# A gated cross-attention layer with routed experts: another start, another order of late loads, and x's normalisation of units 2 to 5 on GpSimd

## What is computed

```python
x = x + tanh(g_xattn) * attention(layernorm(x), ctx)     # 16 heads of 16, 77 context rows, masked
x = x + tanh(g_ffn) * ffn(layernorm(x))
# ffn: softmax(xf @ gate_w.T) -> the best 2 of 4 experts, weights rescaled to sum 1
y = sum over the 2 chosen e of w_e * (silu(xf @ eg[e].T) * (xf @ eu[e].T)) @ ed[e].T
y = y + (silu(xf @ sg.T) * (xf @ su.T)) @ sd.T           # the shared expert
```

## Time and profile before

| | |
|---|---|
| median of 3 runs | 926.68 us (924.75 to 927.69) |
| the profiled execution | 928.73 us, its span 926.8 us |
| busy in the span | TensorE 879.2 us (95%), VectorE 579.7 (63%), ScalarE 478.2 (52%), GpSimd 468.4 (51%) |
| mean granted clock of TensorE | 0.99 of 2.4 GHz |
| chain that ended last, by engine | TensorE 80%, ScalarE 7%, VectorE 6%, issue 3%, DMA 2%, GpSimd 1% |

### The profile page before, as it was taken

One profiled execution on the slowest core, in us unless ns is written; L12 is line 12 of the kernel. 1 busy time (PEld: TensorE's weight loads), 2 busy tenths in 40 slices (PEclk: granted clock), 3 DMA queues, 4 the chain that ended last, 5 costly groups with the idle time before them and its releaser, 6 DMA issues.

```text
span 926.8 us, 22188 instructions
## 1 busy us (share of the span) xinstructions
PE 879.2 (95%) x6635; PEld 786.4 (85%) x6636; DVE 579.7 (63%) x1294; ACT 478.2 (52%) x1804; POOL 468.4 (51%) x644
## 2 busy tenths in 40 slices
PE   6788999999999999799999999999999999999995
PEld 4557788878887899799989999999999999999994
DVE  4788899999988589478654444444444444444442
ACT  2999999999998344366533232323232222222221
POOL 4476667667647334466324444444444444444442
PEclk9899999999999999899999999999999999999998
DMA  7124322223212221333322222222222222222222
GB/s 207 35 78 121 111 87 92 86 63 112 74 59 92 92 76 59 97 99 113 121 58 40 39 41 37 42 37 43 36 44 35 44 35 44 34 45 34 45 34 24
DMA packets 56864, 61.74 MB, mean 67 GB/s; under 512 B 15642, under 2 KB 45183, under 8 KB 56799
## 3 DMA queue, kind: packets, MB, share of 16 engines
q1 hardware_dynamic: 42871, 43.15, 14.8%
q0 software_dynamic: 12864, 17.57, 11.8%
q10 hardware_dynamic: 1064, 0.21, 0.1%
HBM read 34.78 MB, written 25.82 MB: 65 GB/s over the span
## 4 chain that ended last, share of the span: by engine, by line
PE 80%; ACT 7%; DVE 6%; issue 3%; DMA 2%; POOL 1%; SPq 0%; DVEq 0%; POOLq 0%; ACTq 0%
PE p_s L345 27%; PE p_t L355 13%; PE p_f L2410 7%; PE p_f L369 5%; ACT prob L1221 4%; PE p_f L2455 4%; PE p_t L2341 3%; PE p_s L2410 3%; PE p_m L2308 2%; PE p_s L2327 2%; PE p_m L2368 2%; PE p_m L2356 2%; PE p_t L359 2%; PE p_m L330 2%; PE p_s L2455 2%
## 5 line engine op out<-in xcount | busy, mean ns | idle before, releaser
L210 POOL DMA_INDIRECT out_rows<-yout,add_at x67 | 107.2, 1600 | 196.6 <-DVE yout L288 193.5
L1221 ACT ACTIVATE prob<-p_s,negmax 128x77 f32<-128x77 f32 x512 | 164.2, 406 | 3.2 <-DVE negmax L1738 3.1
L295 DVE TENSOR_TENSOR hid<-p_s,sil 128x688 f32<-128x688 f32 x67 | 58.6, 874 | 163.1 <-ACT sil L248 97.9
L248 ACT ACTIVATE sil<-p_s 128x688 f32<-128x688 f32 x67 | 49.9, 744 | 193.6 <-PE p_s L345 193.6
L1221 ACT ACTIVATION_READ_ACCUMULATOR prob<-p_s,negmax 128x1 f32 x512 | 134.8, 289 | 0.0
L884 POOL TENSOR_TENSOR prob<-prob,rinv 128x616 f32<-128x616 f32 x64 | 78.6, 1236 | 74.8 <-DVE rinv L1745 74.8
L345 PE MATMUL p_s<-wgu_hi,fxT_hi 128*128 x402 | 110.7, 384 | 0.0
L345 PE MATMUL p_s<-wgu_lo,fxT_hi 128*128 x402 | 105.5, 371 | 0.0
L345 PE MATMUL p_s<-wgu_hi,fxT_lo 128*128 x402 | 105.5, 370 | 0.0
L259 ACT ACTIVATE hT_hi<-p_f 128x512 fp32r<-128x512 f32 x66 | 39.6, 600 | 122.7 <-PE p_f L369 122.7
L355 PE MATMUL p_t<-wd_hi,hT_hi 128*128 x330 | 98.3, 298 | 0.0
(11 more groups left out here) (283 smaller groups left out, 2442.5 us busy)
## 6 DMA issues: line engine op xcount, KB each, us to landing
xr<-in_x SPq DMA_DIRECT2D x16, 256.0 KB, 3.0
x_scratch<-xr SPq DMA_DIRECT2D x16, 256.0 KB, 2.8
xn_scratch<-xn SPq DMA_DIRECT2D x16, 256.0 KB, 2.2
xt_scratch<-xnT SPq DMA_DIRECT2D x16, 256.0 KB, 2.7
xin<-xt_scratch SPq DMA_DIRECT2D x16, 256.0 KB, 3.3
x1in<-x_scratch SPq DMA_DIRECT2D x16, 256.0 KB, 3.2
out_rows<-syout SPq DMA_DIRECT2D x16, 256.0 KB, 2.2
raw<-in_L_ffn_ed SPq DMA_DIRECT2D x4, 688.0 KB, 4.0
```

Of the source, the lines that this page charges most:

```text
L210: pool.indirect_dma_start(out, bass.IndirectOffsetOnAxis(add_at[k][:, :], 0), yout[k][:, :], None, compute_op=ALU.add).then_inc(s_add, 16)
L248: act.activation(sil[:, :], p_gu[:, 0:FF], ACT.Silu).then_inc(s_sil, 1)
L295: nc.vector.tensor_tensor(hid[:, 0:FF], p_gu[:, FF:2 * FF], sil[:, :], ALU.mult).then_inc(s_hid, 1)
L1221: last = act.activation(prob[n % 2][t][:, m * PW + h * SK:m * PW + (h + 1) * SK], p_s[:, 2 * t + h // 4, col:col + SK], ACT.Exp, bias=negm ...
```

## The change

It has three parts.

1. **Start.** TensorE first makes 20 transposes of the identity into `p_t`, which nobody reads, as soon as the identity is there. All context transposes come ahead of batch 0's keys. ScalarE copies `xT` before it rounds the keys. Rounds 0 and 1 of unit 0's maxima, and round 0 of its exponentials, come ahead of a block `rest_of_start()` that holds what stood before them: keys of batches 1 to 3, statistics and normalisation of unit 1, the gate weights.
2. **Late loads.** SyncE's list for units 7 to 15 is written as one loop with the expert matrices of a unit ahead of the store of the unit before, except in unit 12.
3. **Units 2 to 5.** `normed(2)` to `normed(5)` leave ScalarE. GpSimd makes them, right behind `rstd1(n)`, as x * rs and then + nb, each one instruction of 128x512.

```diff
+            for n in range(WARM):                                  # pe; WARM = 20
+                nc.tensor.transpose(p_t[:, n % 4 * P:(n % 4 + 1) * P], ident[:, :], ident[:, :])
             pe.wait_ge(s_ctx, 16)
...
+            for k in range(KC):
+                for b in range(1, B):
+                    last = nc.tensor.transpose(p_f[k][:, (b - 1) * SK:b * SK], ctx_sb[:, b, k * P:(k + 1) * P],
+                                               ident[0:SK, 0:SK])
             last.then_inc(s_ctxps, 1)
...
             keys_of(0, 1, p_s[:, 1, :])
-            for k in range(KC):
-                for b in range(1, B):
-                    last = nc.tensor.transpose(p_f[k][:, (b - 1) * SK:b * SK], ctx_sb[:, b, k * P:(k + 1) * P],
-                                               ident[0:SK, 0:SK])
-            last.then_inc(s_ctxps, 1)
             x_T(0)
...
             normed(0)
+            xT_copy(0)
             act.wait_ge(s_kT, 2)
             act.activation(kTs[0][:, :, 0:SK], kT[:, :, 0:SK], ACT.Copy).then_inc(s_khi, 1)
-            xT_copy(0)
...
-            act.wait_ge(s_kT, 4)
-            act.activation(kTs[0][:, :, SK:B * SK], kT[:, :, SK:B * SK], ACT.Copy).then_inc(s_khi, 1)
-            normed(1)
+            def rest_of_start():
+                act.wait_ge(s_kT, 4)
+                act.activation(kTs[0][:, :, SK:B * SK], kT[:, :, SK:B * SK], ACT.Copy).then_inc(s_khi, 1)
+                normed(1)
             def first_steps():
                 exps(0, 0)
+                rest_of_start()
                 exps(0, 1)
...
-                normed(2)
...
+            def normed_early(n):
+                par = n % 2
+                pool.wait_ge(s_rs1, n + 1)
+                wait(pool, s_xT, n)
+                wide = [P, UT, H]
+                pool.tensor_tensor(xh[:, :, :], xr[:, n % XR, :, :], rs[0][:, par, :].unsqueeze(2).broadcast_to(wide),
+                                   ALU.mult).then_inc(s_scaled, 1)
+                pool.wait_ge(s_scaled, n - 1)
+                pool.tensor_tensor(xh[:, :, :], xh[:, :, :], nb[0][:, par, :].unsqueeze(2).broadcast_to(wide),
+                                   ALU.add).then_inc(s_xh, 1)
...
                 rstd1(2)
+                normed_early(2)
                 normalise(0, 1)
...
                 rstd1(3)
+                normed_early(3)
                 next_keys(1, 0)
...
-            load_rows(LATE + 1)
...
+            for n in range(LATE, NU):
+                if has(n + 1) and n != NU - 3:
+                    load_rows(n + 1)
+                if n != NU - 4:
+                    experts_of(n)
+                store_y(n - 1)
+                if has(n + 1):
+                    load_x1(n + 1)
+                if n == NU - 4:
+                    load_rows(n + 2)
+                    experts_of(n)
```

More of the change, by code:

```diff
@@ L33 @@
 GW_AT = 480
+WARM = 20
 TOPK = 2
@@ L601, in attend_share_route @@
             "s_consts", "s_iota", "s_pool_chain", "s_p", "s_ex", "s_tot", "s_base", "s_route"))
-        s_weights, s_lgT = sem("s_weights"), sem("s_lgT")
+        s_weights, s_lgT, s_scaled = sem("s_weights"), sem("s_lgT"), sem("s_scaled")
         s_spread, s_row, s_til, s_val, s_vid, s_vlo, s_table = (sem(n) for n in (
@@ L824, in _ @@
                 step(i)
-            load_rows(LATE + 1)
-            def rows_of(n):
-                store_y(n - 1)
-                if has(n + 1):
-                    load_x1(n + 1)
-                if has(n + 2):
-                    load_rows(n + 2)
             def experts_of(n):
@@ L836, in experts_of @@
                         expert_matrix(q)
-            for n in range(LATE, NU - 3):
-                rows_of(n)
-                experts_of(n)
-            for n in range(NU - 3, NU):
-                experts_of(n)
-                rows_of(n)
+            for n in range(LATE, NU):
[9 more added lines that the diff above has]
+                    experts_of(n)
             for q in range(2, 3 * E):
@@ L1008, in first_steps @@
                 rstd1(4)
+                normed_early(4)
                 next_keys(2, 1)
@@ L1016, in first_steps @@
                 rstd1(5)
+                normed_early(5)
                 normalise(3, 0)
@@ L1338, in first_steps @@
                 exps(1, 2, HH // 2)
-                normed(3)
                 exps(1, 3)
@@ L1356, in first_steps @@
                 w_hi(8)
-                normed(4)
                 exps(2, 3)
@@ L1373, in first_steps @@
                 xn_copy(1)
-                normed(5)
                 exps(3, 2, HH // 2)
@@ L1821, in _ @@
             nc.vector.tensor_copy(ctxT[:, :, 0:SK], cols(p_s[:, 0, 0:KC * SK])).then_inc(s_ctxT, 1)
+            dve.wait_ge(s_ctxps, 2)
+            for k in range(KC):
+                nc.vector.tensor_copy(ctxT[:, k, SK:B * SK], p_f[k][:, 0:(B - 1) * SK]).then_inc(s_ctxT, 1)
             dve.wait_ge(s_bias, 48)
@@ L1831, in _ @@
                 key_hi(m)
+            no_sight(0)
             q_lo(0)
-            no_sight(0)
-            dve.wait_ge(s_kps, 2)
-            dve.wait_ge(s_gwps, 1)
-            keys_T(p_t, 1, B)
-            dve.wait_ge(s_gwT, 1)
-            nc.vector.tensor_copy(gwT[:, :, 0:E], p_t[:, GW_AT:GW_AT + KC * E].rearrange("p (c e) -> p c e", e=E)).then_inc(s_gwT, 1)
-            stats_1(1)
             def context_values(k):
@@ L1844, in context_values, with rest_of_start @@
                                         bv[:, :].unsqueeze(1).broadcast_to([SK, 2, H]), ALU.add).then_inc(s_vall, 1)
-            dve.wait_ge(s_tg, 2)
-            nc.vector.tensor_scalar(bog[:, :], bog[:, :], tgx[:, :], None, ALU.mult).then_inc(s_bog, 1)
-            nc.vector.tensor_scalar(tgfh[:, :], tgf[:, :], 0.5, None, ALU.mult).then_inc(s_tgh, 1)
-            dve.wait_ge(s_tgh, 1)
+            def rest_of_start():
+                dve.wait_ge(s_kps, 2)
+                dve.wait_ge(s_gwps, 1)
+                keys_T(p_t, 1, B)
+                dve.wait_ge(s_gwT, 1)
+                nc.vector.tensor_copy(gwT[:, :, 0:E], p_t[:, GW_AT:GW_AT + KC * E].rearrange("p (c e) -> p c e", e=E)).then_inc(s_gwT, 1)
+                stats_1(1)
+                dve.wait_ge(s_tg, 2)
+                nc.vector.tensor_scalar(bog[:, :], bog[:, :], tgx[:, :], None, ALU.mult).then_inc(s_bog, 1)
+                nc.vector.tensor_scalar(tgfh[:, :], tgf[:, :], 0.5, None, ALU.mult).then_inc(s_tgh, 1)
+                dve.wait_ge(s_tgh, 1)
             def first_steps():
                 half_max(0, 0)
+                half_max(0, 1)
+                rest_of_start()
                 context_values(0)
                 context_values(1)
-                half_max(0, 1)
                 stats_1(2)
@@ L2523, in _ @@
                 last = nc.tensor.transpose(p_s[:, 0, k * SK:(k + 1) * SK], ctx_sb[:, 0, k * P:(k + 1) * P], ident[0:SK, 0:SK])
+            last.then_inc(s_ctxps, 1)
+            for k in range(KC):
+                for b in range(1, B):
+                    last = nc.tensor.transpose(p_f[k][:, (b - 1) * SK:b * SK], ctx_sb[:, b, k * P:(k + 1) * P],
+                                               ident[0:SK, 0:SK])
             last.then_inc(s_ctxps, 1)
```

2 lines of the change are left out of this document (removed).

## The result

| | before | after |
|---|---|---|
| median | 927.18 us (924.75 to 928.72, 4 runs) | 918.11 us (915.92 to 918.62, 4 runs) |
| profiled execution, its span | 928.73, 926.8 us | 915.92, 914.2 us |
| ratio of the medians | | 0.990, 95% interval 0.9873 to 0.9927 |

The change saves 9.1 us, about 1%. Forecast were 12.2. The new time is 3.6 us above the forecast of 914.5, and inside its range. Two more measurements of the changed kernel gave 917.77 and 917.61, so this is no accident of one median. The two profiled executions differ by more, 12.6 us of span.

The account below looks back on a forecast made before the run. ScalarE was taken to bound 34 to 84 us, and TensorE from 100 us on, with one 6.21 us hole. The terms -8.5 - 1.1 - 2.6 = -12.2 us took 926.68 to 914.5 us, range 909.5 to 920.0.

Parts of the forecast that it names:

- The hole ahead of `e_T(11)`: TensorE's longest wait behind the start, 6.21 us for matrix 3, which SyncE's queue held behind unit 9's store.
- the size of part 2, taken as -8.5: The reordered late loads end the wait for matrix 3 and the half-rate clock behind it: -8.5 us, bounds -6.2 and -8.9.
- the 6.21 us go: Matrix 3, issued at 362.4 us, lands at 369.8, before `e_T(11)` wants it at 373.6, so TensorE's 6.21 us wait disappears.
- the 2.3 us for the clock: Work behind TensorE's wait, from 380 to 385 us, no longer runs at half clock: 2.3 us, chosen between 1.9 and 2.7.
- The cold case of the prediction: At the start, unit 0's queries stay at half rate and end at 15.2 us; round 1 ends at 28.6: +0.9 us.
- The forecast -1.1: At the start, with queries at full rate, ScalarE ends round 1 at 26.6 us against 27.78: -1.1 us.
- Part 3, taken as -2.6: Moving normalisation of units 2 to 5 from ScalarE to GpSimd gives -1.1 - 0.2 - 1.3 = -2.6 us, bounds -5.2 and +1.0.
- Unit 3: GpSimd's pair delays `normalise(1, 1)` to 51.2 us and `prob_T(1, 0)` to 51.9, giving back 1.2 of 1.4 us: -0.2.
- units 4 and 5: GpSimd's pairs stand ahead of `normalise(n-2, 0)` or `(n-2, 1)`; these units keep half of their 2.7 us: -1.3.
- Early gains lost, the late one stays: 918: Rival: GpSimd's in-order list makes TensorE wait in units 3 to 5, or queries stay at 1.2 GHz: 918 us, chance 0.22.
- GpSimd as the bound: Rival: in units 2 to 5 GpSimd's eight wide instructions, slowed by VectorE, bound the first stretch: 931.2 us, chance 0.02.
- Late waits for `xin`: Rival: loads for units 10, 12 or 13 land later than their cover, each opening a hole: 919.5 us, chance 0.08.

Follow-up runs that it names:

- The run with one number changed: The kernel before with only matrix 3's entry in the table AFTER_UNIT changed from 10 to 9: 919.93 us, ratio 0.9934.
- the two other kernels: The kernel before with only the new start, 926.15 us, and the kernel before with only units 2 to 5 normalised by GpSimd, 924.64 us.

## Why the prediction was right, and where it was not

**Right: the sign, and what carries it.** The hole ahead of `e_T(11)` was the largest gain, the queue's order held it, and it went for the price that was named (waits for `xin` on ScalarE, none on TensorE). The run with one number changed shows that matrix 3 is all of it, as far as these runs can tell. The total came out inside the range with the largest term too large and a start that isn't told from nothing, so it has to be judged by its terms.

**Wrong by 1.8 to 2.3 us: the size of part 2, taken as -8.5.** The step was "the 6.21 us go" and the 2.3 us for the clock. In the executions of the old order that were traced, late is 659.2, 656.4 and 655.7 us and 649.4 to 650.2 in the new: against the middle of these, 649.8, that is 9.4 us for the traced execution of before, and 6.6 and 5.9 for the two others; the medians of the two kernels say 6.7 and 6.2. The wait depends on when the matrix could be issued (372.41, 371.06 and 372.26 us) and on how long it took to land (7.4, 6.0 and 5.1 us), and the trace read was that of before's slowest execution. The forecast saw that this execution lay 2.05 above the median and took 2.05 off, but priced the hole at its worst length. An execution that is 2 us slow is slow somewhere, and here it was slow in the very wait that the change removes, so part of these 2.05 was taken off twice. Before itself was traced only once, so that the hole is shorter in its other executions is concluded from the two other kernels and from the medians. Both bounds, -6.2 and -8.9, came from that same execution; the lower one is near the value measured, but only because the clock's part was left out of it.

**Wrong: "I take it that after 20 transposes and the context the engine is at full rate for unit 0's queries".** They took 3.37 to 3.75 us (forecast 2.0) in every trace. In the changed kernel's first trace the granted clock fell between 9 and 10 us (0.94 over that us, 0.50 from 10.0 on), while TensorE waited for ScalarE's `xT`; in the two others it fell between 8 and 9 us (0.70 and 0.68), while TensorE was busy all of the time. The rule of the Trainium skill ("TensorE: Matmul & The Clock Gate", Part 1), that activity releases the throttle, agrees with the keys' 1.09 us in four of the eight traces with the transposes; in two others the keys took 1.96 us behind the same transposes. That its release would last until the queries was my reading, and the traces contradict it. The cold case of the prediction stood at +0.9, and such starts were measured: +1.2 with the transposes, +1.0 without. The forecast -1.1 was measured as well, in the good starts. What failed is that these are not two cases with one true, but executions of one program, and the median is between: 0.0 alone, 1.0 worse on top of part 2 (920.58 against 919.53), 0.9 better with all three (917.77 against 918.64). These signs differ by less than the intervals; part 1 isn't told from nothing.

**Part 3, taken as -2.6: 1.6 alone, and the 2.5 of one pair needs the clock.** With the new start it gave 2.5 us in one pair of traces, and 2.5 to 3.0 by the medians (920.58 against 918.11, 917.77 and 917.61, from different groups); alone it gave 1.6, which lies amid the 1.1 to 1.9 of its units at equal clock. Unit 2 is as forecast (1.0 for 1.1). Unit 3 is as forecast too (0.2, measured +0.3 to -0.3 at equal clock), and by the mechanism named: where the clock was up, `prob_T(1, 0)` waited 0.95 and 1.15 us for GpSimd. Its time was wrong in detail, since the sum left GpSimd's step where it was: the start and unit 2 moved it ahead by 1.7 and 1.0 us, and a wide instruction takes 1.04 us in place of 1.26, so `normalise(1, 1)` ended near 48.2 or 49.2 and not at 51.2. The term that was mis-sized is that of units 4 and 5: forecast at 1.3 (half of 2.7), they gave 0.4 to 0.6, all of it unit 4's. That the sum of -2.6 is met by the 2.5 of one pair is luck: 0.9 of it arose where the granted clock was 0.79 against 0.63.

**The rivals.** "Early gains lost, the late one stays: 918" has the number that was measured, 918.11, but not the mechanism: early, the changed kernel's three traces lead before's by 2.9, 2.3 and 1.8 us, and the late gain is 2 us smaller. "GpSimd as the bound" didn't come: between 20 and 100 us TensorE waits for `prob` from GpSimd for 1.0, 2.3 and 1.0 us in all in the changed kernel's three traces. Its contention had no place either: the wide instructions took 1.038 to 1.041 us each, so nothing that VectorE did slowed one of them, and the rule that was named beside it (the Trainium skill, "SBUF — State Buffer", Who interferes with whom) had no price in these eight. "Late waits for `xin`" came only on ScalarE.

**What would show it wrong** was listed as: a new wait of over 2 us in units 9 to 13 (one of 2.93 us, on ScalarE and covered), GpSimd as releaser of more than 3 us (2.3 at most), queries of unit 0 at 3.7 us (yes, 3.37 to 3.75), and a lead at 100 us more than 3 us off 3.7 (it is 2.9, 2.3 and 1.8 in the traces, by unit 6's queries and unit 15's alike). The third told true, and its price was the start. The first came to the letter as well, but the covered wait wasn't on the path. Of the signs of being right, two failed beside the queries: a wide instruction takes 1.04 us and not 1.3, and TensorE's wait ahead of `prob_T(1, 0)` came in one of the three traces of the changed kernel only.

## What to carry to other kernels

Price a hole from more than one execution: a wait for a transfer that is only just too late varies with the transfer's issue and landing, and where the profiled execution lies above the median, look whether the excess sits in such a hole. Where a queue holds one urgent load behind a store that waits, look for the smallest edit of its order first; here one number in a table had all of it. And before giving an early lead a price of one us, see whether the clock in that stretch does the same in two executions of the same program, and compare traces with the same clock there.
